# Attention scores as stacked bfloat16 products in 64-row strips, with the expert tiles half a sequence later

## The reference, cut to what matters

```python
def ffn(x, w_qkv, w_o, ...):           # x: 16 x 256 x 128, H = 16 heads, hd = 8
    qkv = x @ w_qkv
    q, k, v = jnp.split(qkv, 3, axis=-1)
    q, k, v = (to_heads(q), to_heads(k), to_heads(v))
    scores = jnp.einsum('bhqd,bhkd->bhqk', q, k) / jnp.sqrt(jnp.float32(hd))
    scores = jnp.where(causal, scores, jnp.finfo(scores.dtype).min)
    attn = jax.nn.softmax(scores, axis=-1)
    o = jnp.einsum('bhqk,bhkd->bhqd', attn, v)
    h = layernorm(x + o.transpose(...) @ w_o, g1, b1)
    # top 2 of 8 experts of each row, each expert two matmuls with gelu between
    return layernorm(h + moe, g2, b2)

x = x + 0.5 * ffn(layernorm(x)); x = x + dilated(layernorm(x)) / 4; x = x + 0.5 * ffn(layernorm(x))
```

## Time and profile before

| | us |
|---|---|
| three runs | 1319.13, 1328.95, 1325.6 |
| median | 1325.6 |
| the profiled execution, its own time | 1316.56 |
| its span, first to last instruction | 1314.6 |
| TensorE busy | 1082.5 (82%) |
| VectorE busy | 679.8 (52%) |
| ScalarE busy | 640.3 (49%) |
| GpSimd busy | 567.3 (43%) |

### The profile page before, as it was taken

One profiled execution on the slowest core, in us unless ns is written; L12 is line 12 of the kernel. 1 busy time (PEld: TensorE's weight loads), 2 busy tenths in 40 slices (PEclk: granted clock), 3 DMA queues, 4 the chain that ended last, 5 costly groups with the idle time before them and its releaser, 6 DMA issues. The chain is left out here.

```text
span 1314.6 us, 29449 instructions
## 1 busy us (share of the span) xinstructions
PE 1082.5 (82%) x11041; PEld 866.0 (66%) x11041; DVE 679.8 (52%) x2097; ACT 640.3 (49%) x1379; POOL 567.3 (43%) x708
## 2 busy tenths in 40 slices
PE   1787987799988999889988999889988998794670
PEld 0555655677766777777766877767766776684560
DVE  4445555355547564675546573665546554350313
ACT  0132333475646555555656555555645556552340
POOL 1023237213645335643655335643645336624505
PEclk9798888899988989989999999989988999796795
DMA  5084013545355526444364526445364635485661
GB/s 111 8 168 129 5 31 97 150 145 162 112 163 155 148 83 178 158 123 140 121 174 150 155 90 188 140 124 149 117 170 140 180 118 162 138 266 189 208 218 44
DMA packets 116467, 180.98 MB, mean 138 GB/s; under 512 B 12360, under 2 KB 79464, under 8 KB 116328
## 3 DMA queue, kind: packets, MB, share of 16 engines
q1 hardware_dynamic: 108136, 162.32, 42.6%
q0 software_dynamic: 8192, 16.79, 4.2%
HBM read 145.10 MB, written 38.68 MB: 140 GB/s over the span
## 5 line engine op out<-in xcount | busy, mean ns | idle before, releaser
L748 DVE TENSOR_REDUCE part_max<-ps_quad 128x6 f32<-128x768 f32 x256 | 233.1, 952 | 160.5 <-PE ps_quad L417 160.4
L618 ACT ACTIVATE probs<-ps_quad 128x768 f32<-128x768 f32 x256 | 195.8, 808 | 224.6 <-PE ps_quad L443 224.1
L972 POOL TENSOR_SCALAR_AFFINE_SELECT probs<-probs 128x512 f32<-128x512 f32 x256 | 162.0, 644 | 277.4 <-ACT probs L618 273.1
L654 ACT ACTIVATE act<-ps_ring,weights 128x128 f32<-128x128 f32 x736 | 204.4, 378 | 81.0 <-PE ps_ring L537 80.4
L537 PE MATMUL ps_ring<-tile_t,weights 128*128 128x128 f32 x1472 | 211.4, 292 | 25.8 <-DVE tile_y L877 15.8
L537 PEld LDWEIGHTS ps_ring<-tile_t,weights 128*128 128x128 f32 x1472 | 189.7, 202 | 44.7 <-issue 32.3
L546 PE MATMUL ps_ring<-weights,act 128*128 128x128 f32 x1472 | 214.0, 294 | 1.8 <-ACT act L654 1.4
L546 PEld LDWEIGHTS ps_ring<-weights,act 128*128 128x128 f32 x1472 | 193.0, 205 | 20.3 <-issue 16.4
L977 POOL TENSOR_TENSOR rstd<-var_eps,power 128x4 f32<-128x4 f32 x56 | 57.5, 1026 | 246.8 <-DVE var_eps L704 246.8
L1030 POOL DMA_INDIRECT picked<-sorted_outputs,place x128 | 122.7, 959 | 77.7 <-issue 77.5
L439 PE MATMUL ps_quad<-q4s,k 32*128 32x128 f32 x1024 | 97.6, 339 | 66.3 <-DVE part_max L748 66.2
(11 more groups left out here) (130 smaller groups left out, 1432.5 us busy)
## 6 DMA issues: line engine op xcount, KB each, us to landing
weights<-expert_weights SPq DMA_DIRECT2D x184, 578.0 KB
tile_rows<-sorted_rows SPq DMA_DIRECT2D x56, 192.0 KB, 5.7
sorted_outputs<-tile_y SPq DMA_DIRECT2D x56, 192.0 KB, 2.9
query_key_parts<-qk SPq DMA_DIRECT2D x32, 256.0 KB, 3.5
k<-query_key_parts SPq DMA_DIRECT2D x64, 64.0 KB
q<-query_key_parts SPq DMA_DIRECT2D x64, 64.0 KB
sorted_rows<-zeros SPq DMA_DIRECT2D x2, 1472.0 KB, 10.9
xs<-in_L_attn_x SPq DMA_DIRECT2D x8, 256.0 KB, 7.8
```

The costliest lines, as they stand in the source:

```text
L618: sc.activation(probs[:, r % PROBS, 2 * a:2 * a + 2, :], ps_quad[:, 2 * a:2 * a + 2, 0:3 * P], ACT.Exp, scale=HD ** -0.5).then_inc(pair_fr ...
L654: ins = sc.activation(act[:, k % ACTS, f, :], bank(use)[:, f * P:(f + 1) * P], ACT.Gelu_apprx_tanh, bias=weights[:, k % WEIGHTS, 2 * F + f ...
L748: dve.tensor_reduce(part_max[:, :, heads, j].rearrange("p c i -> p i c"), ps_quad[:, heads, 0:3 * P].rearrange("p i (c k) -> p i c k", c=3 ...
L972: pool.affine_select(out=both, in_=both, compare_op=ALU.is_ge, fill=0.0, base=0, pattern=[[0, 2], [0, 2], [1, P]], channel_multiplier=-1). ...
```

## The change

1. Queries and keys are split into three bfloat16 parts each (high, middle, low), and the product is taken as six products of parts: 6 x 8 features are stacked in 48 rows, and 16 more rows hold the shift, so a head has 64 rows. `exps` multiplies 64 rows, `scores` 48. A quad is now two pairs of 64-row strips. Each matmul is one bfloat16 instruction in place of two.
2. The split: ScalarE copies the projection to bfloat16 (`project`), VectorE subtracts (`rest`), ScalarE copies (`middle`), VectorE subtracts (`low`), each 128x512, for queries and for keys.
3. `spread` becomes `spread_out` (six transfers for each of queries and keys, a part going to up to three places) and `spread_in` (two transfers of 48x4096).
4. The shift is not added to the queries: VectorE splits the maxima in two (seven small operations, was two), TensorE turns them, ScalarE copies them to `shift_rows`, and SP copies these into the 16 shift rows of `q_stack` with two transfers (`shift_in`). `exps(n, 0)` waits for these.
5. `shift` goes from slot misc_3 to weigh_0 of the same half; `turn` and `project` go from misc_1, misc_2, misc_3 to scores_0, second_a, misc_1.
6. Expert tiles of a set, and all behind them, come one half later; the program has one half more.
7. At the start: half of the constant rows of the keys and the bias are made later (`keys_rest`, `bias`), the zeroing of `values` goes to GpSimd, zeroing of `q4` is gone.

```diff
-        put(2 * n - 1, "misc_3", ("shift", n))
+        put(2 * n - 1, "weigh_0", ("shift", n))
+        put(2 * n - 1, "first_a", ("shift_in", n))
...
-            half = first + 13 + q
+            half = first + 14 + q
...
-            def spread(m, which):
...
-                sp.dma_start(rows, qk[:, which, :]).then_inc(parts_out[which], 16)
...
-                for i in range(4):
-                    sp.dma_start(into[32 * i + 4:32 * i + 4 + HD, m % 2, :, :], of_head[i]
...
+            def spread_out(m, which):
+                sp.wait_ge(split_ready[which], m + 1)
+                for i in range(STRIPS):
+                    for part, to in enumerate(PLACES[which]):
+                        rows = parts[m % 2, which, i, to].rearrange("n d j t -> (d j) n t")
+                        sp.dma_start(rows, qk[STRIP * i:STRIP * (i + 1), which, part, :].unsqueeze(1).broadcast_to(
+                            [STRIP, rows.shape[1], TOK])).then_inc(parts_out[which], 16)
+
+            def spread_in(m, which):
...
+                sp.wait_ge(parts_out[which], 16 * STRIPS * 3 * (m + 1))
+                for i in range(STRIPS):
+                    sp.dma_start(into[STRIP * i:STRIP * i + STACK, m % 2, :, :],
+                                 parts[m % 2, which, i].rearrange("n d j t -> (n d) j t")
                                  ).then_inc(parts_in[which][m % 2], 16)
+
+            def shift_in(n):
+                freed(sp, ("shift", n))
...
+                    sp.dma_start(q_stack[rows, n // 2 % 2, :, n % 2 * S:n % 2 * S + S],
+                                 shift_rows[rows, n % 2, :].unsqueeze(1).broadcast_to([STRIP - STACK, PAIRS, S])
+                                 ).then_inc(shifted[n % 2], 16)
...
             def exps(n, j):
...
                 if j == 0:
-                    freed(pe, ("shift", n))
+                    pe.wait_ge(shifted[n % 2], 16 * STRIPS * (n // 2 + 1))
                 for a in range(2):
                     pe.wait_ge(pair_free[a], QUAD_NO["exps", n, j])
...
+                    q, k = q_stack[:, par, 2 * j + a, at:at + S], k_stack[:, par, 2 * j + a, at:at + S]
+                    for i in range(STRIPS):
+                        rows = slice(STRIP * i, STRIP * (i + 1))
+                        pe.matmul(ps_quad[:, 2 * a + i, 0:P], k[rows, P:S], q[rows, P:S], start=True, stop=True,
+                                  tile_position=(STRIP * i, 0))
...
+            def rest_of(m, which):
...
+                dve.tensor_tensor(rest[:, which, :], bank(("project", m, which)), qk[:, which, 0, :], ALU.subtract
+                                  ).then_inc(free_sem(("project", m, which)), 1)
+
+            def low(m, which):
+                dve.wait_ge(split_mid[which], m + 1)
+                dve.tensor_tensor(qk[:, which, 2, :], rest[:, which, :], qk[:, which, 1, :], ALU.subtract
+                                  ).then_inc(split_ready[which], 1)
...
-                dve.tensor_tensor(q4s[:, n % 2, :, :], q4[:, n // 2 % 2, :, n % 2 * S:n % 2 * S + S],
-                                  bank(use)[:, 0:S].unsqueeze(1).broadcast_to([P, GROUPS, S]), ALU.add
```

More of the change, by code:

```diff
@@ L38 @@
 WEIGHTS = 6
-KEPT = 6
 ACTS = 4
@@ L386, in project @@
                 take(pe, use)
-                pe.matmul(bank(use), wqkv[:, which * D:(which + 1) * D], xn_t[:, :], start=True, stop=True
+                pe.matmul(bank(use), w_qk[:, which, :], xn_t[:, :], start=True, stop=True
                           ).then_inc(ring_full, 1)
@@ L670, in long_scores @@
                               ).then_inc(free_sem(use), 1)
[L672 to L679 removed]
+            pieces = {"bias": bias, "turn": turn, "project": project, "middle": middle, "exps":
+                      exps, "shift": shift, "weigh": weigh, "merge": merge,
+                      "gate": gate, "turn_tiles": turn_tiles, "first": first, "long_turn":
+                      long_turn, "long_scores": long_scores}
             for kind, *at in ORDER:
@@ L953, in _ @@
-            ins.then_inc(const_dve, 1)
-            pieces = {"norm": norm, "norm_apply": norm_apply, "project": project, "values": project_values,
-                      "scores": scores, "shift": shift, "rows": rows, "attn_out": attn_out, "mid_norm": mid_norm,
+            step(dve.tensor_reduce(pair_rows[:, :], row_of[:, STACK:STRIP].rearrange("p (j c) -> p j c", c=2), AX.X,
+                                   ALU.add))
+            settle()
+            for j in range(PAIRS):
+                ins = dve.tensor_scalar(k_stack[:, 0, j, :], pair_rows[:, j:j + 1].broadcast_to([P, TOK]), -1.0, None,
+                                        ALU.mult)
@@ new lines, in _ @@
+            ins.then_inc(keys_set, 1)
+            dve.wait_ge(w_in, 16)
+            for which in range(2):
+                ins = dve.tensor_copy(w_qk[:, which, :].rearrange("p (i d j) -> p i d j", i=STRIPS, d=HD),
+                                      w_given[:, which * D:(which + 1) * D].rearrange("p (j i d) -> p i d j", j=PAIRS,
+                                                                                      i=STRIPS))
+            ins.then_inc(weights_turned, 1)
+            pieces = {"keys_rest": keys_rest, "norm": norm, "norm_apply": norm_apply, "rest": rest_of, "low": low,
+                      "values": project_values,
+                      "scores": scores, "rows": rows, "attn_out": attn_out, "mid_norm": mid_norm,
```

268 lines of the change are left out of this document (149 added, 119 removed).

## The result

The changed kernel is slower: 1365.9 us median (1362.2 to 1368.6, 4 runs) against 1325.5 us (1319.1 to 1329.0, 4 runs) for the kernel before beside it, a ratio of 1.031 (95% interval 1.026 to 1.036), +40 us. The forecast was 1247 us, range 1200 to 1302. The profiled execution of the changed kernel has a span of 1366.9 us against 1314.6 before.

A forecast was written before the change was run, and what follows sets the result against it. TensorE's own list of work was taken to set the pace from 50 to 1138 us. Terms -100 - 24 - 7 + 14 + 10 + 18 + 10 = -79 take 1316.6 to 1238; 9 more for the median gives 1247 us, range 1200 to 1302.

The forecast's parts named there:

- under 190 us: Sign of success: lines of scores and exps busy less than 190 us together, a quad 0.54 us at full clock.
- what it is worth: Time saved by faster scores and exps matmuls on TensorE: 93 us, divided by a clock of 0.93, -100 us.
- tiles later: Expert tiles half a sequence later: fewer TensorE waits for tile rows, -24 us, and one batch moved into a gap, -7 us.
- ScalarE behind exps: In halves with tiles, ScalarE's table load and exponentials make TensorE wait in `scores_1`: 0.3 us in some 47 halves, +14 us.
- stall behind GpSimd: VectorE waits for GpSimd's product of `end_rows`; TensorE arrives some 1.4 us earlier at this stall, seven times: +10 us.
- shift by transfer: Shift rows by ScalarE copy and transfer: 12 us late before the tiles, 6 us for late ones, together +18 us.
- the rest, and the clock: Added VectorE, ScalarE, SP and DMA work not hidden beside TensorE, and a slightly lower clock: +10 us.
- start: Ahead of the first scores: added split operations and longer transfers, offset by constants made later: 0 us.
- three signs named for being wrong: Quads above 0.7 us; waits for maxima or exponentials up by more than 50 us; attention-stage clock near 0.8.
- evacuation rival: TensorE waits for VectorE or ScalarE emptying `ps_quad`; half the quads' saving goes into waits: 1297 us, chance 0.15.
- clock rival: With less work the busy share falls and TensorE's clock drops to 0.85 through the attention: 1321 us, chance 0.07.
- shift-rows rival: Shift rows arrive late at `exps(n, 0)` in every sequence, 5 us each: 1372 us, chance 0.06.

The follow-up runs named there:

- e10: Kernel before, with the matmuls of the first half of each exponentials' quad issued twice: 1363.5 us, ratio 1.030 to the kernel before.
- e2: Changed kernel with every matmul of scores and exps issued twice: 1395.2 us, ratio 1.053 to the kernel before.
- e8: Kernel before, with only the expert tiles and what follows them half a sequence later: ratio 0.990 to the kernel before.
- e3: Changed kernel with the expert tiles and what follows moved back a half sequence, as before: 1407.1 us, ratio 1.063 to the kernel before.
- e6: Changed kernel with the last addition (end_add) and its store half a sequence later: ratio 1.005 to the kernel before.
- e15: Kernel before, with only the last addition and its store half a sequence later: 1304.0 us, ratio 0.985 to the kernel before.
- e4: Changed kernel with `rest` put ahead of `combine` in VectorE's list: 1340.3 us, ratio 1.014 to the kernel before.
- e1: Changed kernel with the expert-weight packing cut in three, behind the shift rows of sequences 1, 2 and 3: 1333.4 us, ratio 1.007 to the kernel before.
- e16: e12 with the matmuls of scores and exps issued twice: ratio 1.013 to the kernel before, 2.7% over e12.
- e9: Changed kernel with row maxima over the first 64 of each 128 keys: 1317.0 us, ratio 0.995 to the kernel before.
- e13: Kernel before, with row maxima over the first 64 of each 128 keys: ratio 0.969 to the kernel before.
- e12: Changed kernel with three moves (packing later, `rest` ahead of `combine`, last addition later): 1306.7 us, ratio 0.986 to the kernel before.
- e11: Kernel before, with expert tiles half a sequence later and the last addition and store another half later: 1296.0 us, ratio 0.980 to the kernel before.
- e5: Changed kernel with six writes of query and key parts a job in place of twelve, layout changed: ratio 1.026 to the kernel before.
- e14: e12 with row maxima over the first 64 of each 128 keys: ratio 0.950 to the kernel before.
- e7: Changed kernel with the edits of e1, e4, e5 and e6 together: ratio 0.997 to the kernel before.

## Why the prediction was wrong

Its terms, in its own order:

| step | predicted | measured |
|---|---|---|
| busy time of the quads | under 190 us, quad 0.54 us | 253.6 us by line (before 405.9), as one and with the masks 156 us less; quad 0.43 us |
| what it is worth | -100 us | added quad time costs 76% of itself in the kernel before (e10), 34% in the changed one (e2) |
| tiles later | -31 us | -1.0% alone (e8); its undoing +41 us (e3) |
| ScalarE behind exps | +14 us | waits for `probs` 17.0 us, 40 times (before 3.6) |
| stall behind GpSimd | +10 us | some +14: 34 us there now (e6), of which the kernel before had 20 (e15) |
| shift by transfer | +18 us | waits 51.5 us; 20 without the one of 31.5 |
| the rest, and the clock | +10 us | `rest` 26 us (e4); parts of queries and keys wait 83 us (before 17) |
| start | 0 | +6 us at n = 0, +38 at n = 1, 32 of it the packing (e1) |
| clock | above 0.88 | 0.842 |

**The step that failed first** is the reading of the bound. From 181 busy of 200 us I concluded that TensorE's own list sets the pace, and turned saved time into time one to one; I even divided by the clock, to get 100. The saving in busy time was larger than that, 156 us. But what e10 measures is 76% in the kernel before, and e2 and e16 measure 34 and 43% with the saving made. TensorE was the fullest engine of a loop in which VectorE, ScalarE and GpSimd each had a share: shortening VectorE by 102 us brings 3.1 to 3.6% in every version. With TensorE's part shorter, it arrives at each hand-over earlier and waits there. The sentence in the prediction that a round takes 5.0 us while the loop of a pair needs 4 says how near the next limit was, and I used it against the rival.

**The second** is that an order written by hand was read only near the moved pieces, and the start was put at nothing. `spread_out`, `rest` and `shift_in` were put into queues, and I counted the twelve writes and looked at weights and stores, but not at `pack`, which follows `spread_in` of job 1 on SP: 33 us of issuing ahead of the shift rows (32 us by e1). Nor did I look at what stands ahead of `rest` on VectorE (`combine`, 26 us by e4). The prediction had asked itself which pieces wait behind a late `exps`, but not what a piece new to a queue waits behind.

**A step that held** is the stall at `end_add`: the term was what the change adds, 10 us, and 34 us now against 20 before are some 14. What I overlooked is that the kernel before already loses 1.5% there (e15), a gain that needed no stacked scores.

**A misreading that changed no term** is the "1.59 us each" for a quad: it divides the sum of four lines that overlap, while the quads took 0.88 us at full clock. The sign "under 190 us" does not fit the prediction's own saving either, since 405.9 less 93 is 313. And none of the three signs named for being wrong came: quads stayed below 0.7 us, the waits for maxima and exponentials grew by 19 us, and the clock of the steady stage was 0.87 to 0.90.

The shift by transfer came out right in its sum, apart from the packing, and by luck: the waits without the longest are 20.0 us, 18 were predicted. But 12 of these were to lie before the expert tiles, where only the wait of the packing stands; all 20.0 lie behind 240 us, where 6 were expected, and e1, with the packing gone, has no such wait before 240 us either. ScalarE was right: 13 us more, against 14. The share of DMA was as predicted in the steady stage (0.59 to 0.65 against 0.59).

Of the rivals, none is what happened. The evacuation rival let half of the saving go into waits; in the steady stage all of it went. Its mechanism, waits for maxima and exponentials wherever a piece is short, is at most (71.9 - 66.2) + (17.0 - 3.6) = 19 us. The Trainium skill's page "TensorEngine Tiling (Array Packing)" (Performance Considerations, PSUM Bottleneck) says that tiling leaves the emptying of PSUM as slow as it was; e9 and e13 agree that the emptying costs time (3.5 and 3.1% for 102 us of it), and add that it cost as much without the stacks. The clock rival's numbers came true in part: 0.88 where 0.97 stood before. The clock goes with the idle time: in e2, with more work in the same order, it is 0.91 instead of 0.88 between 750 and 950 us, and behind the wait at 614 us matmuls take twice their time. The shift-rows rival gave the nearest time (1372 us) for the wrong reason: it put 5 us in every sequence, and there was one wait of 31.5 us.

**What stays open.** The account of the steady stage is read from the traces, not shown by runs one by one. Setting e12 beside e11, TensorE's idle time (55 us more) and its other matmuls (10 us longer) take 65 of the 78 us that the quads save, and the waits lie on seven and more releasers; that the crowded order as a whole does it is my reading. A rival that no run took away is the work that came with the stacks: VectorE is busy 25 us and ScalarE 33 us more than before. At the 0.4 to 0.5 us that a microsecond of VectorE's reductions was worth, VectorE's part is some 11 us, an estimate; ScalarE's price was not measured. The largest wait is also untouched: for the parts of queries and keys TensorE waits 93.3 us in e12, 75 of them before 470 us, where e11 has 19.2. In the same time e12 falls 25 us behind e11 (17 by n = 4). The forecast gave the parts no term of their own, only 3 us at the start, and no run shortened their way.

## What to carry to other kernels

An engine that is busy 90% of a stretch need not be the whole bound, nor stay it: issue its suspected work twice, and halve that of its neighbour, before paying for a faster version of it; here the two probes said 76% for TensorE and 43% for VectorE before the change, and 34% and 48% once it was made. Lines that run side by side must be taken as one before their busy times are compared: added up, e2 seemed to add 185 us where it added 86. Whenever a piece moves into a queue (SP's above all), list everything that this queue issues ahead of it in the whole program, one-time work too, with its duration. And try the free moves of order first: two of them gave 2.0% on the kernel before, and the stacked scores with their three moves gave 1.4%.

## What was not expected of the hardware

Two strips with two heads each in bfloat16 take 0.43 us a quad, less than the fixed 0.20 us and 0.34 us of streaming that I had worked out; so the 0.20 us was not fixed. The issue of a write of `query_key_parts` on SP takes 612 ns at the median where it took 340 before, and from issue to landing the transfers of these parts take 4.6 to 12.8 us, 8.5 at the median (before 2.0 to 5.7, 3.5). And chips differ: on the chips of e5 to e8 and of e13 and e14 the kernel before took 1388 and 1390 us, 5% more, while VectorE's reduction took 952 ns there as elsewhere. Every trace taken on those chips has waits to which no releaser is found, and no other trace has one over 1 us. In e8 a reduction starts 3.6 us after the end of the mask matmuls that it needs:

```profile
214.28 1.03 PE L417 MATMUL ps_quad<-causal,ident_bf 128*128 128x256 bf16 x4
...
218.88 1.82 DVE L748 TENSOR_REDUCE part_max<-ps_quad 128x6 f32<-128x768 f32 x2 [9.28 <-remote]
```

Why is not known. It makes the waits read in e5 to e8, e13 and e14 less sure than the others. Each ratio was taken on one chip, and comparisons of ratios between chips (e7 with e12) are weaker than the intervals say.
